# A recommender tower on one core: VectorE block transposes in place of two trips through DRAM, last layers by single tiles, gram matrices ahead of them

## The reference

```python
x = layer_norm(dense_t @ Wd.T, gd, bd)                     # 128 per sample
y = layer_norm(einsum('bnd,ed->bne', sparse_t, Ws), gs, bs)  # 26 x 128
y = einsum('bne,pn->bep', y, Wsi)                          # 26 features mixed to 32
y = layer_norm(y, gsi, bsi)                                # over the 32
T = concatenate([x[:, None, :], swapaxes(y, 1, 2)], axis=1)  # 33 x 128
Z = einsum('bnd,bmd->bnm', T, T)                           # the gram matrix
out = layer_norm(Z[:, TRIL_I, TRIL_J] @ Wl.T, gl, bl) * mask # 528 -> 512, first 384 kept
h = relu(concatenate([z, dense], 1) @ W_top1 + b_top1)     # 640 -> 512
h = relu(h @ W_top2 + b_top2)                              # 512 -> 256
return h @ W_top3                                          # 256 -> 1
```

## Time and profile before

| | |
|---|---|
| median of 3 runs | 1138.94 us (1137.81 to 1141.31) |
| the profiled execution's own time | 1137.1 us |
| its span, first to last instruction | 1135.3 us |
| mean granted TensorE clock | 0.773 of full |
| gathers on GpSimd | 416, 396.7 us busy |

### The profile page before, as it was taken

One profiled execution on the slowest core, in us unless ns is written; L12 is line 12 of the kernel. 1 busy time (PEld: TensorE's weight loads), 2 busy tenths in 40 slices (PEclk: granted clock), 3 DMA queues, 4 the chain that ended last, 5 costly groups with the idle time before them and its releaser, 6 DMA issues.

```text
span 1135.3 us, 16073 instructions
## 1 busy us (share of the span) xinstructions
PE 633.2 (56%) x6573; PEld 465.5 (41%) x6573; DVE 458.6 (40%) x627; ACT 250.4 (22%) x530; POOL 397.4 (35%) x422
## 2 busy tenths in 40 slices
PE   2125417262655529364491836827286461998886
PEld 1123305141434317153370624525164341766675
DVE  3239607252343316252270603706055150585600
ACT  0211103031222105030240302303032120343411
POOL 6735560707162440706226071351705325000000
PEclk9999658576776759676695757958588575998999
DMA  5103220305030500305021140302303041024010
GB/s 158 26 13 78 55 58 8 80 21 127 9 81 11 135 16 16 73 20 125 11 56 36 27 120 6 73 19 70 82 1 77 14 117 26 2 66 108 2 52 1
DMA packets 109129, 58.96 MB, mean 52 GB/s; under 512 B 91248, under 2 KB 99584, under 8 KB 107392
## 3 DMA queue, kind: packets, MB, share of 16 engines
q1 hardware_dynamic: 94928, 43.16, 15.6%
q0 software_dynamic: 13312, 13.66, 5.8%
q10 hardware_dynamic: 816, 1.11, 0.3%
HBM read 38.47 MB, written 19.42 MB: 51 GB/s over the span
## 4 chain that ended last, share of the span: by engine, by line
PE 42%; issue 28%; another core or an unknown queue 16%; DVE 7%; ACT 5%; SPq 1%; DMA 1%; ACTq 0%; DVEq 0%
PE L L433 7%; PE b_y L367 7%; PE L L415 6%; PE b_a L348 6%; PE b_z L379 5%; PE b_mix L357 3%; PE L L439 3%; DVE var_y L747 2%; PE b_a L339 2%; ACT embt L492 1%; DVE yb L740 1%; DVE ro L779 1%; SPq L203 1%; ACT layers L485 1%
## 5 line engine op out<-in xcount | busy, mean ns | idle before, releaser
L296 POOL DMA_INDIRECT emb<-in_tbl,idx x416 | 396.7, 954 | 560.1 <-DVE nrm L734 435.5
L379 PE MATMUL b_z<-V 128*32 128x34 f32 x4096 | 96.7, 203 | 205.7 <-issue 205.2
L752 DVE RECIPROCAL rstd_y<-std_y 128x32 f32<-128x32 f32 x64 | 22.5, 352 | 407.4 <-ACT std_y L512 406.6
L348 PE MATMUL b_a<-gram_w,embt 128*128 128x128 f32 x416 | 82.1, 351 | 180.7 <-ACT embt L492 171.8
L379 PEld LDWEIGHTS b_z<-V 128*32 128x32 f32 x4096 | 67.5, 112 | 253.5 <-issue 250.3
L348 PEld LDWEIGHTS b_a<-gram_w,embt 128*128 128x128 f32 x416 | 69.0, 247 | 192.5 <-ACT embt L492 180.6
L519 ACT ACTIVATE zs<-b_z 128x272 f32<-128x272 f32 x64 | 40.8, 638 | 427.5 <-remote 259.9
L507 ACT ACTIVATE sq<-yb 128x1024 f32<-128x1024 f32 x64 | 67.7, 1057 | 157.1 <-DVE yb L740 129.8
L357 PE MATMUL b_mix<-mix,byn 128*128 128x128 f32 x512 | 86.0, 310 | 28.2 <-issue 27.9
L367 PE MATMUL b_y<-mixed,projw 64*128 64x512 f32 x256 | 88.6, 774 | 10.8 <-ACT mixed L502 10.8
L747 DVE TENSOR_REDUCE var_y<-sq 128x32 f32<-128x1024 f32 x64 | 77.8, 1216 | 38.4 <-ACT sq L507 36.1
(11 more groups left out here) (109 smaller groups left out, 564.2 us busy)
## 6 DMA issues: line engine op xcount, KB each, us to landing
by_sample<-nrm SPq DMA_DIRECT2D x16, 832.0 KB
byn<-by_sample SPq DMA_DIRECT2D x64, 208.0 KB
emb<-in_tbl,idx POOLq DMA_INDIRECT x416
zt<-rows SPq DMA_DIRECT2D x8, 640.0 KB
dense<-in_r_dense_t SPq DMA_DIRECT2D x8, 256.0 KB
rows<-zs SPq DMA_DIRECT2D x32, 64.0 KB
rows<-zs SPq DMA_DIRECT2D x32, 48.0 KB
V<-in_L_rec_Wl ACTq DMA_DIRECT2D x1, 1056.0 KB
```

The source lines that it names most:

```text
L296: pool.indirect_dma_start(out=emb[t % 2][:, f, :], out_offset=None, in_=tables[f], in_offset=bass.IndirectOffsetOnAxis(ap=idx[:, t, f:f + ...
L348: last = nc.tensor.matmul(b_a[:, n * P:(n + 1) * P], embt[:, n, :], gram_w[:, :], start=True, stop=True)
L379: last = nc.tensor.matmul(b_z[32 * q:32 * q + 32, GRAM * j:GRAM * (j + 1)], v[:, 0:NP], v, start=True, stop=True)
```

## The change

Both trips through DRAM go. `nrm` is written in an order that lets VectorE transpose 32x32 blocks straight into `byn`, and `zs` is turned the same way by three block transposes into `zb`, after which TensorE transposes it (`pair_rows`). A tile's normalization is split in two halves (14 and 12 features), and GpSimd's run of 26 gathers is split likewise: the first 14 wait for the first half, the last 12 for the second, two quarters later. The last layers run on one tile of 128 samples at a time, over four quarters; the product with `wlt` has the samples as weights and 512 moving columns. The moments of `x` and of the interaction come from `bn_stats` on VectorE. In a quarter TensorE does gram before every last layer; ScalarE takes `deviation_y` at the head of the next quarter and `copy_zs` a quarter later. Projection starts one quarter earlier (h = 4t+6), and there are 83 quarters instead of 84.

```diff
-LAG_B, LAG_ROWS, LAG_L = 7, 16, 19
+HALVES = [range(0, 14), range(14, 26)]
+MEASURE = 1
+DENSE = 2
+DENSE_NORM = 3
+DENSE_BACK = 4
+SHUFFLE = 5
+PROJECT = 6
+PAIRS = 12
+INTERACT = 13
+INTERACT_NORM = 14
+INTERACT_BACK = 15
+LAYER1 = 18
+LAYER2 = 20
+LAYER3 = 21
+STORE = 22
...
-                after(pool, nrm_ready, t - 1)
                 for b in range(4):
+                    after(pool, nrm_ready, 2 * (t - 2) + b // 2 + 1)
                     for f in features(b):
...
+            def shuffle(t):
+                dve.wait_ge(nrm_ready, 2 * (t + 1))
+                after(dve, mix_done, 4 * (t - 1))
+                for k in range(2):
+                    d = slice(k * D // 2, (k + 1) * D // 2)
+                    nc.vector.transpose(byn[t % 2][:, :, d].rearrange("p j d -> p d j"), nrm[:, d, :]).then_inc(byn_ready, 1)
...
+            def by_sample(t):
+                dve.wait_ge(zs_copied, 4 * (t + 1))
+                after(dve, zt_done, 2 * t)
+                src = zs[t % 2]
+                nc.vector.transpose(window(zb, (ND - 1) * NP, (1 - NP, ND), (NP, NP)), src[:, 0:ND, :]).then_inc(zb_ready, 1)
...
+            def interact(t):
+                pe.wait_ge(zt_copied, 2 * (t + 1))
+                for c in range(RC):
+                    last = nc.tensor.matmul(b_l1[:, :], zt[:, c, :], wlt[:, c, :], start=(c == 0), stop=(c == RC - 1))
```

More of the change, by code:

```diff
@@ L106, in tower @@
[L106 to L120, removed]
@@ L443, in output, with dense_transposes @@
-            def output(g):
-                pe.wait_ge(h2_relued, 2 * (g + 1))
+            def dense_transposes(t):
+                pe.wait_ge(dense_loaded[t % 2], 16 * (t // 2 + 1))
+                if t == 0:
+                    pe.wait_ge(mixw_ready, 1)
+                after(pe, x_copied, 2 * t)
+                after(pe, zt_copied, 2 * (t - 2))
+                for f in range(2):
+                    last = nc.tensor.transpose(b_x[:, f * P:(f + 1) * P], dense[t % 2][:, f * P:(f + 1) * P], ident[:, :])
+                last.then_inc(x_transposed, 1)
@@ new lines, in dense_project, with dense_back @@
+            def dense_project(t):
+                if t == 0:
+                    pe.wait_ge(wdt_ready, 1)
+                pe.wait_ge(dt_copied, t + 1)
+                for f in range(2):
+                    last = nc.tensor.matmul(b_x[:, 2 * P:3 * P], dt[t % 5][:, f, :], wdt[:, f, :], start=(f == 0), stop=(f == 1))
+                last.then_inc(x_projected, 1)
+            def dense_back(t):
+                pe.wait_ge(xn_done, t + 1)
+                nc.tensor.transpose(b_x[:, 3 * P:4 * P], xn[:, :], ident[:, :]).then_inc(xt_done, 1)
@@ new lines, in pair_rows @@
+            def pair_rows(t):
+                pe.wait_ge(zb_ready, 3 * (t + 1))
+                after(pe, zz_copied, t)
+                for c in range(4):
+                    last = nc.tensor.transpose(b_l0[:, c * P:(c + 1) * P], zb[:, ZB_PAIR + c * P:ZB_PAIR + (c + 1) * P], ident[:, :])
+                last.then_inc(zt_done, 1)
+                pe.wait_ge(x_copied, 2 * min(t + 3, T))
+                nc.tensor.transpose(b_x[0:64, 0:P], zb[:, ZB_X:ZB_X + 2 * NP], ident[:, :], tile_position=(0, 0))
+                nc.tensor.matmul(b_x[64:96, 0:P], ones[:, 0:32], xt[t % 3][:, :], start=True, stop=True, tile_position=(0, 64)).then_inc(zt_done, 1)
@@ L786, in _ @@
             prepare()
             for h in range(QUARTERS):
-                ab, bc, cc = measured(h), projected(h), projected(h - 1)
-                i, x = dense_step(h)
-                g, k = layer_step(h)
+                ab, bc, cc = part(h, MEASURE), part(h, PROJECT), part(h, PROJECT + 1)
+                if (t := tile(h, PAIRS)) is not None:
+                    by_sample(t)
+                if (t := tile(h, INTERACT_NORM)) is not None:
+                    moments_o(t)
+                if (t := tile(h, DENSE_NORM)) is not None:
+                    moments_x(t)
+                    normalize(t, 0)
```

744 lines of the change are left out of this document (363 added, 381 removed).

## The result

The changed kernel takes 1053.93 us (median of 4 runs, 1047.75 to 1059.32) beside 1138.38 us for the kernel before: a ratio of 0.925, 95% interval 0.918 to 0.932. The forecast was 1160 (1095 to 1205): wrong in sign, and out of its range.

A forecast was written before the change was run, and what follows sets the result against it. Gathers were taken to hold the engines, each tile's hold and free stretch running in series. Changes of -12, +13, +43 and -16 gave +28 us on 1137.1, 1165; 1160 was named, range 1095 to 1205.

The forecast's parts named there:

- The cycle in series: Per tile: a hold (first gather to release of the engines), then a free stretch; before, 36.9 + 31.2 = 68.1 us.
- half a quarter each, one quarter per tile: TensorE's work inside the two holds: one quarter per tile instead of about 0.6.
- I take the whole: Release after each run's last gather: the full 5.6 us, making holds of 22.0 and 19.5, 41.5 us against 36.9.
- The forecast of the cycle: Time per tile: 71.5 us, taken between ends of 69.1 and 73.4.
- The faster rival: Holds priced by what they catch: free stretch 24.9, cycle 66.4, 1109 us, or 1085 with shrinking release; chance 0.36.
- my own sum of quarters: Free stretch summed row by row, 17.2 + 4.4 + 6.4 + 3.9 = 31.9 us; the forecast itself had chance 0.35.
- three signs: Would prove the forecast wrong: gram undisturbed in a short run, release under 5 us, free stretches under 28 us a tile.
- Start and end: Up to tile 2's first gather -12 us; after tile 15's first gathers -31 + 15 = -16 us.
- The term between them: From tile 2 to tile 5: last layers start earlier and each tile has two holds, +13 us.
- VectorE's transposes: shuffle 2.4 to 3.8 us, free inside a hold, 34 us or more without that cover; by_sample 1.3 to 2.0 us.
- The rival of GpSimd held up by transposes: A VectorE transpose stops gather issue for its length, 14 x 3.1 = 43 us, total 1204; chance 0.05.
- The slower sign: Whole kernel: the change makes it slower than before; chance 0.55.

The follow-up runs named there:

- j4: Changed kernel with gram behind the last layers, VectorE's block transposes behind the scaling, and gathers for the first two tiles only: 713.6 us, ratio 0.634 to the kernel before.
- h4: Changed kernel with TensorE's gram behind the last layers again and VectorE's block transposes of nrm behind the scaling into V: 1028.77 us, ratio 0.914 to the kernel before.
- j2: Changed kernel with gram last, transposes behind the scaling, and gathers released as four runs of 8, 6, 6 and 6 per tile: 985.67 us, 0.877 of before.
- j1: Changed kernel with gram last, transposes behind the scaling, and all 26 gathers of a tile in one run: 1088.93 us, ratio 0.967 to the kernel before.
- h3: Changed kernel with only VectorE's block transposes of nrm moved behind the scaling into V: 1044.08 us, ratio 0.928 to the kernel before.
- m2: Changed kernel with each 512-column product with wlt cut into four of 128 columns: 726.57 us, ratio 1.056 to the kernel before, in a set without holds.
- f1: The changed kernel itself, unedited, in a set without holds: 725.56 us, ratio 1.053 to the kernel before.
- e3: Changed kernel with only TensorE's gram put back behind the last layers, in a set without holds: 669.69 us, ratio 0.973 to the kernel before.
- m3: Changed kernel with gram last, transposes behind the scaling, and gathers in eight groups of 3 or 4, in a set without holds: 667.06 us, 0.971 of before.

## Why the prediction was wrong

**The cycle in series, right.** Hold and free stretch follow one another: two holds a tile, each ending after its last gather. Gathers are the cause: without them the tile falls from 60.4 to 35.3 us (j4 against h4). They hold only on some sets of runs, which the one trace of before could not show.

**The step that failed: "half a quarter each, one quarter per tile".** I took it that a hold lets half a quarter pass, and put the rest of it behind the release, 4.4 us for layer 1 and 6.4 for the product with `wlt` and layer 3. The trace has both inside the holds, and part of the next quarter: 16.4 us of TensorE's work a tile instead of 9.6. Without those 10.8 us my free stretch of 31.9 is 21.1; measured are 23.1. Nor does a hold begin at the head of a quarter: at 510.55 the quarter's transposes and mix are behind and its norms nearly so, and what the hold takes in is the projection, gram, the last layers and the next quarter's transposes and mix.

The reading of the earlier trace rows behind it was wrong. In a run of 26 little passes over 37 us, and I spread that evenly. But in the held traces other than j2's VectorE ends its last piece in a hold at most 10.9 us after the first gather (15.3 in one hold), and TensorE creeps from about 7 us on, here through its caught gram in the kernel before:

```profile
321.74 2.86 PE L415 MATMUL L<-zt,wlt 128*128 128x256 f32 x12
...
330.03 0.32 PE L379 MATMUL b_z<-V 128*32 128x34 f32 x3 [1.19 <-issue]
...
343.47 0.22 PE L379 MATMUL b_z<-V 128*32 128x34 f32 x1 [1.88 <-issue]
```

And what a hold lets through is a number of passes that does not grow with the run: 81 to 99 with a run of 26 before, 87 to 93 with one of 26 in j1, 87 and 87 to 97 with the runs of 14 and 12 after, 99 and 80 to 95 in h4 (holds from 250 us on). A quarter has some 105, so a hold lets most of a quarter through, not half, and a run cut in two does so twice: 1.7 quarters a tile, not one. (Only j2 has more, up to 191.) Where TensorE then stops, it waits for a copy by ScalarE, which itself waits for one of TensorE's late signals: after the second hold above the copy into `embt` starts at 528.24 and TensorE's next matmul at 528.75. That this is why the number stays the same is my reading; no run tests it.

**"I take the whole" 5.6 us of release, wrong in size.** It is 3.6 us after 14 gathers and 2.7 after 12, 4.9 less than the two times 5.6. The runs themselves are 1.8 us a tile longer than at a pitch of 1.26 (17.3 and 14.7 us). The holds are 38.4 us a tile, not 41.5. The bound below of that sum, 36.9, was named, but the value taken was the upper.

**The forecast of the cycle** was 71.5 us, the measured one 61.3 (490.36 / 8). The faster rival (0.36) had the mechanism: the hold priced by what is caught in it, 24.9 us free, a release that shrinks by 1.3 us a run. It gave 63.8 us and 1085 (by its own terms, 1109 less 10 x 2.6, 1083); of the 2.5 us by which that cycle is still too long, 1.8 are in its free stretch. It had the right argument for it in the earlier trace rows, TensorE nearly full in free stretches. I gave it 0.36, no more than my own sum of quarters (0.35), which had no row for what passes in a hold, and the forecast went by the sum. All three signs that I had named against the forecast came: a gram nearly undisturbed, a release earlier than 5 us, free stretches under 28 us a tile.

**Is it the split, the trips or the layers?** On held chips two runs against one are 5.3 points (j1, h4). The whole change less this and less the loss by gram ahead (1.3 points, h3 and h4) leaves 7.3 - 5.3 + 1.3 = 3.3 points (0.967 of j1) for missing trips, new last layers, start and end together. On the kernel before the split alone gives only 1.9. So the larger part is the split in the new kernel, and how the small part is shared between trips and layers is open. The traces say where to look. TensorE's busy time inside a tile's holds is 10.2 us before, 14.5 in j1 and 20.1 in h4 (means of ten tiles); one tile of j1 and one of h4:

```profile
409.94:447.47 37.53, 13.41 (x95) 7.62 (x93) 9.12 (x9) 1.21 (x2) 25.57 (x26) 0.63 0.12 23
```

```profile
471.83:492.60 20.77, 8.69 (x103) 6.66 (x99) 6.44 (x9) 2.21 (x6) 14.24 (x14) 0.66 0.12 23
503.07:521.74 18.67, 11.43 (x98) 6.97 (x98) 9.52 (x10) 2.38 (x5) 11.63 (x12) 0.76 0.11 22
```

The split adds 5.7 us. The 4.3 us before it come with as few passes as before, but with the ten long ones of 512 columns among them. If a hold counts passes and not work, long passes are a gain of their own; m2 was to test that, and only its time in a held set would show it.

**Start and end.** -12.9 us at the start for -12. At the end -8.4 for -16. Both held in sign. The term between them did not: from tile 2 to 5 it was -5.8 us for +13; the two holds a tile stood in it as a cost.

**VectorE's transposes.** `shuffle` is 3.67 us, at the top of 2.4 to 3.8; `by_sample` 1.05 + 1.01 + 0.20 = 2.3, above 2.0. They were hidden, as said (h3). The estimate of 5.0 us from the Trainium skill, "VectorE: DVE Perf Modes", section "The three transpose paths", is too high for these blocks of 32 bits.

**The rival of GpSimd held up by transposes falls:** the gathers issued beside them took 0.94 to 0.95 us (510.55 to 513.05 above). Beside the scaling into `V` the one at 514.30 took 1.91 us, and so did all 27 gathers that begin during such a scaling in this trace (1.75 to 1.99). Such a gather ends 0.8 us after the scaling does, so the cost is what is left of the scaling: in the kernel before, where 0.4 us was left at most, it took up to 1.19 us. One that begins during `nrm` with more than 0.25 us of it left ends 0.7 us after it (f1, e3).
**The slower sign** was right only where gathers hold nothing (1.053), and it was not my reason that made it so. VectorE's transposes ahead of `V`, which I had at nothing inside a hold and at 34 us or more without its cover, put gram 3.98 us late each tile; with gram last the whole 56 us are gone (e3).

## What to carry to other kernels

A stall that comes with a burst of transfers has a shape in time: before pricing a change that splits the burst, read from the windows and the timeline what passes in its first third and what in its last, count the instructions and not only the time, and don't carry the mean of a long burst over to two short ones. When a term is free because a stall hides it, price it without the stall too, since the stall may be absent: here the same change was 7.5% faster with it and 5.3% slower without. The version with gram last and the transposes late was faster in both (h4, 0.914; m3, 0.971).

## What the hardware showed

- Indirect gathers held the other engines in some sets of runs and not in others, with the same program: 1126 to 1138 us or 688 to 689 us for the kernel before. The issue of a gather is the same, 0.94 us at a pitch of 1.25 where nothing delays it. What sets the state is unknown.
- TensorE's signals are what comes late in a hold. By the semaphore events of the changed kernel, the gram that ended at 542.92 us is signalled 9.87 us later, and of the 26 grams that ended during a run of gathers 25 came 7.7 to 9.9 us late (one 25.3); outside runs it is 0.01 to 0.05 us, and in f1_after never over 0.32, gathers or not. In j1, with runs of 26, it is 6.3 to 23.8 us.
- Without holds GpSimd is busy or issuing without a break in the faster versions: in e3_gram_last the last gather is issued at 569.5 us, and no wait but "issue" stands before 415 of the 416. It is not the only bound: the tile takes 35.5 us there, and 35.3 in j4, which has no gathers by then.

```profile
POOL emb L253 <- issue: 126.5, 415, 0.3
```
